# A hand-scheduled attention and FFN kernel: attention steps moved, five instruction streams put in a run-time loop, another warm-up

## The reference

```
a   = layernorm(x)
xn  = layernorm(a) * gamma + beta
q, k, v = split(xn @ w_qkv)            # 4 heads of 32
k   = softmax(k, over tokens);  q = q / sqrt(32)
att = (q @ (k^T v)) @ w_out + b_out + a
x   = x + layernorm(att)
f   = sum over 8 experts of (silu(n @ Wg) * (n @ Wu)) @ Wd,  n = layernorm(x)
x   = x + layernorm(f)
```

## Time and profile before

| what | value |
|---|---|
| median of 3 runs | 551.97 us |
| the profiled execution's time | 551.86 us |
| its span in the trace | 550.1 us, 8657 instructions |
| PE busy | 542.4 us |
| DVE busy | 446.2 us |
| ACT busy | 347.5 us |
| POOL busy | 168.4 us |

### The profile page before, as it was taken

The page is one execution under the profiler, slowest core; times in us unless marked ns, Lnnn a source line. Parts: engine busy times, 40 slices in busy tenths (PEclk is TensorE's granted clock), DMA queues, the critical chain, the costliest instruction groups (busy, mean ns, idle before and its releaser), DMA issues.

```text
span 550.1 us, 8657 instructions
## 1 busy us (share of the span) xinstructions
PE 542.4 (99%) x2633; PEld 467.3 (85%) x2633; DVE 446.2 (81%) x982; ACT 347.5 (63%) x626; POOL 168.4 (31%) x205
## 2 busy tenths in 40 slices
PE   9999999999999999999999999999999999999996
PEld 5687888888888888888888888888888888888885
DVE  5897897899769997799877988779976898778666
ACT  6778776756675566755658566675667555655554
POOL 4888691216203360034501335022520033001001
PEclk9999999999999999999999999999999999999999
DMA  5433020210102101111102011021010200010000
GB/s 176 143 88 115 20 58 2 77 44 15 59 0 78 57 20 40 40 37 59 43 16 73 24 40 58 0 78 39 20 39 1 77 20 21 19 40 0 21 1 19
DMA packets 28030, 24.47 MB, mean 44 GB/s; under 512 B 3024, under 2 KB 20944, under 8 KB 27984
## 3 DMA queue, kind: packets, MB, share of 16 engines
q1 hardware_dynamic: 27408, 23.73, 13.6%
q10 hardware_dynamic: 576, 0.20, 0.1%
HBM read 15.27 MB, written 8.65 MB: 43 GB/s over the span
## 4 chain that ended last, share of the span: by engine, by line
PE 94%; DVE 2%; ACT 1%; issue 1%; POOL 0%; POOLq 0%; DVEq 0%; ACTq 0%
PE gate_ps L1033 10%; PE acc_ps L1036 10%; PE acc_ps L1034 10%; PE gate_ps L1034 10%; PE gate_ps L1036 10%; PE acc_ps L1033 10%; PE up_ps L1034 10%; PE up_ps L1033 10%; PE up_ps L1036 10%; PE att_ps L1119 1%; PE att_ps L1130 1%; PE up_ps L1178 1%; PE att_ps L1092 1%; DVE h L839 0%; DVE h_lo L826 0%
## 5 line engine op out<-in xcount | busy, mean ns | idle before, releaser
L623 ACT ACTIVATE gs<-gate_ps 128x512 f32<-128x512 f32 x255 | 152.0, 596 | 175.6 <-PE gate_ps L1036 173.3
L839 DVE TENSOR_TENSOR h<-gs,up_ps 128x512 f32<-128x512 f32 x255 | 174.5, 684 | 90.5 <-PE up_ps L1036 88.7
L826 DVE TENSOR_TENSOR h_lo<-h,h_hi 128x512 fp32r<-128x512 f32 x255 | 195.6, 767 | 0.1
L600 ACT ACTIVATE h_hi<-h 128x512 fp32r<-128x512 f32 x255 | 158.9, 623 | 10.4 <-DVE h L839 9.9
L1033 PE MATMUL gate_ps<-x1nT_hi,wg_hi 128*128 128x512 f32 (+1 forms) x256 | 100.1, 391 | 0.0
L1036 PE MATMUL gate_ps<-x1nT_lo,wg_hi 128*128 128x512 f32 (+1 forms) x256 | 96.9, 379 | 0.0
L1033 PE MATMUL up_ps<-x1nT_hi,wu_hi 128*128 128x512 f32 (+1 forms) x256 | 96.9, 379 | 0.0
L1034 PE MATMUL gate_ps<-x1nT_hi,wg_lo 128*128 128x512 f32 (+1 forms) x256 | 96.9, 379 | 0.0
L1036 PE MATMUL up_ps<-x1nT_lo,wu_hi 128*128 128x512 f32 (+1 forms) x256 | 96.9, 379 | 0.0
L1034 PE MATMUL up_ps<-x1nT_hi,wu_lo 128*128 128x512 f32 (+1 forms) x256 | 96.9, 379 | 0.0
L1036 PE MATMUL acc_ps<-h_lo,wd_hi 128*128 128x512 f32 x254 | 96.6, 380 | 0.3 <-DVE h_lo L826 0.3
(11 more groups left out here) (238 smaller groups left out, 490.0 us busy)
## 6 DMA issues: line engine op xcount, KB each, us to landing
w_raw<-in_L_ffn_Wg_dram SPq DMA_DIRECT2D x8, 256.0 KB, 2.9
w_raw<-in_L_ffn_Wu_dram SPq DMA_DIRECT2D x8, 256.0 KB, 2.6
w_raw<-in_L_ffn_Wd_dram SPq DMA_DIRECT2D x8, 256.0 KB, 3.1
x_in<-in_L_attn_x_dram SPq DMA_DIRECT2D x7, 256.0 KB, 2.8
t_dram_acc<-t_blk_acc SPq DMA_DIRECT2D x7, 256.0 KB, 2.3
t_out_acc<-t_dram_acc SPq DMA_DIRECT2D x28, 64.0 KB, 2.0
out_dram<-res SPq DMA_DIRECT2D x7, 256.0 KB, 2.0
t_dram_x<-t_blk_x SPq DMA_DIRECT2D x6, 256.0 KB, 2.2
```

What stands on the lines that cost most here:

```text
L600: act.activation(h_hi[s % NH][:, :], h[s % NGU][:, :], ACT.Copy).then_inc(s_hhi, 1)
L623: act.activation(gs[q][:, :], gate_ps[q][:, :], ACT.Silu).then_inc(s_silu, 1)
L826: dve.tensor_tensor(h_lo[s % NH][:, :], h[s % NGU][:, :], h_hi[s % NH][:, :].bitcast(F32), ALU.subtract).then_inc(s_hlo, 1)
L839: dve.tensor_tensor(h[q][:, :], gs[q][:, :], up_ps[q][:, :], ALU.mult).then_inc(s_h, 1)
```

## The change

Three parts. The tables for batches 1 to 7 are rewritten; the FIRST tables stay. `bodies` becomes a run-time loop on each engine: batch 0 unrolled, a loop of two rounds with the bodies of an odd and an even batch (1 and 2, then 3 and 4), then batches 5, 6 and 7 unrolled; some waits are followed by an increment of a semaphore that nobody waits for, so that they are instructions of their own. And the warm-up ahead of the first body is 11 bf16 matmuls, a wait for the first weight part, 6 float32r matmuls with strided views of it and 2 bf16 matmuls, in place of 20 bf16 ones. SP issues the x1n transfers ahead of those of x, and ACT no longer waits for attn before it writes xnT.

```diff
-PE_AT = {"kT": 1, "A": 9, "M": 11, "G": 13, "attn": 14}
-DVE_AT = {"kmax": 2, "acc": 2, "E_T": 3, "next_stats": 6, "A": 10, "fin_stats": 10, "M": 12, "fin_scale": 12, "next_T": 14,
-          "z": 15, "z_stats": 15, "x1_stats": 20, "next_xnT_lo": 22, "x1n_T": 23, "x1n_lo": 29}
-ACT_AT = {"exp": 2, "G": 14, "next_xnT": 20, "next_xnT_hi": 21, "x1n_hi": 28}
-POOL_AT = {"yb": 4, "next_rstd": 7, "next_xn": 10, "fin_rstd": 11, "fin_out": 13, "z_rstd": 16, "x1": 16, "x1_rstd": 20}
-BUSY = {"start": 8, "w": 5, "attn": 20}
+PE_AT = {"kT": 1, "A": 9, "M": 10, "G": 11, "attn": 12}
+DVE_AT = {"next_xnT_lo": 31, "kmax": 2, "acc": 2, "E_T": 3, "A": 10, "fin_stats": 10, "M": 11, "fin_scale": 12, "z": 13, "z_stats": 13,
+          "next_stats": 16, "x1_stats": 18, "x1n_T": 21, "next_T": 24, "x1n_lo": 27}
+ACT_AT = {"exp": 2, "G": 12, "x1n_hi": 26, "next_xnT": 29, "next_xnT_hi": 30}
+POOL_AT = {"yb": 4, "fin_rstd": 11, "fin_out": 13, "z_rstd": 14, "x1": 14, "x1_rstd": 18, "next_rstd": 21, "next_xn": 21}
+BUSY = {"start": 8, "w": 5, "attn": 11, "end": 2}
...
-        def bodies(body):
-            for b in range(B):
-                body(b, b % 2, first=b == 0, nxt=b < B - 2, last=b == B - 1)
+        def wait_alone(eng, semaphore, value):
+            eng.wait_ge(semaphore, value)
+            eng.sem_inc(s_waited, 1)
+        def bodies(eng, body):
+            body(0, 0, first=True, nxt=True, last=False)
+            with eng.Fori(0, (B - 4) // 2) as i:
+                body(i * 2 + 1, 1, first=False, nxt=True, last=False)
+                body(i * 2 + 2, 0, first=False, nxt=True, last=False)
+            body(B - 3, 1, first=False, nxt=True, last=False)
+            body(B - 2, 0, first=False, nxt=False, last=False)
+            body(B - 1, 1, first=False, nxt=False, last=True)
...
         # SP body
                     store(b - 1)
+                    if not last:
+                        store_blocks("x1n", s_x1n_blk, b)
+                        load_blocks("x1n", b)
                 if nxt:
                     store_blocks("x", s_xh_blk, b + 1)
                     load_blocks("x", b + 1)
-                if not first and not last:
-                    store_blocks("x1n", s_x1n_blk, b)
-                    load_blocks("x1n", b)
...
         # POOL: power, scale_of (both waits) and next_xn; DVE: aggregate
-                pool.wait_ge(s_ve[k], count)
+                wait_alone(pool, s_ve[k], count)
-                dve.wait_ge(s_st[k], count)
+                wait_alone(dve, s_st[k], count)
...
         # ACT, next_xnT
-                    act.wait_ge(s_attn_ps, c - 1)
...
         # PE, ahead of the first body
             keep_busy(BUSY["attn"])
+            pe.wait_ge(s_whi, 1)
+            w0, w1 = w_hi[0][:, 0, :], w_hi[0][:, 0, 0:P]
+            forms = [w0.rearrange("p (a b) -> p b a", a=4), w0.rearrange("p (a b) -> p b a", a=8),
+                     w0.rearrange("p (b a) -> p a b", a=2)]
+            for moving in forms:
+                for _ in range(2):
+                    pe.matmul(up_ps[0][:, :], w1, moving, start=True, stop=True)
+            keep_busy(BUSY["end"])
```

More of the change, by code:

```diff
@@ L202, in build @@
         s_made = sem("s_made")
+        s_waited = sem("s_waited")
         s_mask = sem("s_mask")
@@ L425, in body @@
                     load_blocks("x", b + 1)
-                if not first and not last:
-                    store_blocks("x1n", s_x1n_blk, b)
-                    load_blocks("x1n", b)
-            bodies(body)
+            bodies(sp, body)
             sp.wait_ge(s_last_res, JH)
@@ L445, in scale_of @@
             def scale_of(k, c, dst, src, done, which=0, place=range(J)):
-                pool.wait_ge(s_rstd[k], c)
-                pool.wait_ge(s_nm[k], c)
+                wait_alone(pool, s_rstd[k], c)
+                wait_alone(pool, s_nm[k], c)
                 for j in range(J):
@@ L493, in body @@
                             if nxt:
-                                pool.wait_ge(s_A_ps, b + 1)
+                                wait_alone(pool, s_A_ps, b + 1)
                                 attention("xn", b + 2, par)
@@ L538, in _ @@
                 split_lo(pool, m)
-            bodies(body)
+            bodies(pool, body)
             for i in range(2):
@@ L687, in _ @@
             act.activation(blocks_of(x1nT_hi[0][:, :], 1), two(up_ps[2][:, HALF]), ACT.Copy).then_inc(s_x1nT_hi, 1)
-            bodies(body)
+            bodies(act, body)
             last_step()
@@ L993, in _ @@
                 dve.tensor_copy(x1[0][:, j, :], tile_banks[j][:, D:2 * D]).then_inc(s_f_x1, 1)
-            bodies(body)
+            bodies(dve, body)
             last_step()
@@ L1262, in _ @@
                     last.then_inc(s_f_n, 1)
-            bodies(body)
+            bodies(pe, body)
             last_step((B - 1) % 2)
```

## The result

| | before | after |
|---|---|---|
| median of 6 runs each | 552.09 us (551.83 to 552.37) | 555.94 us (555.61 to 556.38) |
| ratio | | 1.0069, 95% interval 1.0057 to 1.0083 |
| profiled execution: time, span | 551.86, 550.1 us | 555.68, 553.9 us |

A forecast was written before the change was run, and what follows sets the result against it. PE was taken as the bound, busy 542.4 of 550.1 us. 551.86 + 2.7 (M to G) + 0.4 (exp chain) + 0.1 (jump) + 0 (warm-up) = 555.1; the median's 0.1 more makes 555.2 us, range 551.5 to 558.2.

The forecast's parts named there:

- exp chain in the loop: Batches 1 to 4: the loop's register work delays the chain from exp to h_lo, and so PE; 0.4 us (0 to 1.2).
- jump back: End of the loop's first round: instruction fetch delays DVE and ACT, covered by their idle time; 0.1 us (0 to 2.7).
- Part 1: Batches 1 to 6: attention stages drawn together, G waits for M_sb behind fin_stats on DVE; 2.7 us (1.8 to 3.6).
- The sign that was named for it: PE waits 0.3 to 0.5 us for M_sb; period 65.9 in late unrolled batches, 66.0 in looped ones, against 65.43.
- Part 2: The next batch's x chain goes late, with SP's new order and ACT's dropped wait; covered by step distances, cost 0.
- rival B: The loop is dear: PE has no lead at the jump, or the exp chain costs 1.2; 557.9 or 558.7 us; chance 0.17.
- rival C: Faster: batch 0's single waits for Ek and h_lo go and G doesn't wait either; 550.8 us; chance 0.10.
- A (G doesn't wait): Not slower: M_sb is ready in time for G in batches 1 to 6, the 2.7 goes; 552.0 us; chance 0.18.
- Part 4: Warm-up before the first transposes: strided matmuls at 0.216 us cost 0; at double that, PE 0.8 late at most.

The follow-up runs named there:

- e9: The kernel before with the new tables, SP's new order and ACT's dropped wait, but fin_stats behind M_sb on DVE: 552.37 us, ratio 1.0001.
- e3: The new kernel with the old warm-up of 20 bf16 matmuls: 555.89 us, ratio 1.0065.
- e6: The kernel before with only the separate waits added, unrolled, old tables and old warm-up: 553.25 us, ratio 1.0017.
- e2: The new kernel with fin_stats moved from DVE's step 10 to 11, behind M_sb: 553.95 us, ratio 1.0029.
- e5: The kernel before with only the new tables, SP's order and ACT's dropped wait, unrolled, old warm-up: 553.38 us, ratio 1.0019.
- e7: The new kernel with ACT's bodies written out and the other engines looped: 555.51 us, one execution.
- e12: The kernel before with batch 0's A one step later on PE and M, G, attn two later: median 556.11 us (two sorts of times), ratio 1.0039.
- e10: The kernel before with A, M, G and attn of batch 0 one step later on PE: 551.79 us, ratio 0.9991.
- e11: As e10, with x_stats, x_rstd and xn of batch 0 also moved to step 4: 552.07 us, ratio 0.9998.

## Why the prediction was right, and where its sum was not

The forecast was 555.2, and 555.94 lies in its range and on its side. Its terms against what the runs give:

| term | forecast | measured |
|---|---|---|
| M to G, its separate wait included | 2.7 (1.8 to 3.6) | 2.0: 0.33 x 6 |
| exp chain in the loop | 0.4 (0 to 1.2) | 0 to 0.1: looped 65.78, unrolled 65.75 |
| jump back | 0.1 (0 to 2.7) | 0.9 |
| x chain late, SP's order, ACT's wait | 0 | 0 (e9) |
| warm-up | 0 (to 0.8) | 0 (e3) |
| batch 0, separate waits | not priced | 0.8 (e6) |

**Part 1** had the mechanism, the place and the number of batches right (e2, e9), and its size 0.12 per batch too high. In e5, without the separate waits, it is 0.2: G 0.09 late and 0.1 of weight loading behind it. I had 0.31 late. Two slips make the difference. M costs PE more than the 0.45 between the end of step 11 (175.56 + 9 x 0.216 = 177.50) and 177.95: the second matmul behind it comes late too, 0.32 behind the first. Before, the row next to those of the earlier trace rows shows it:

```profile
178.27 0.38 PE L1034 MATMUL gate_ps<-x1nT_hi,wg_lo 128*128 128x512 f32 x1
```

There this 0.10 fell into step 12, behind 177.95; with M ahead of step 11 it falls in front of G, so PE wants G at 178.05 (in e9, where G waits for nothing, it comes 5.33 behind A; A at 172.73 before and 5.33 make 178.06). And I took the start of the next DVE instruction, 177.85, for that of `M_sb`; but that h stands 0.18 behind `ve_fin`, and `M_sb` starts 0.08 behind it (179.04 and 179.12 above), so at 177.75, and ends at 178.10. 0.05 behind that is 178.15, 0.10 late, as measured. The separate wait was taken at 0.05 of 0 to 0.15 and is 0.12: the 0.16 of idle that stands ahead of the aggregation.

The sign that was named for it came weaker: G's wait of 0.22 does not stand in the list of PE's waits of the new kernel, and the periods are 65.75 and 65.78 where 65.9 and 66.0 were expected.

**Part 2** held: distances of many microseconds hide the whole x chain. **The register work** held at its lower end. **The warm-up** cost the start 0.31 (first gate matmul at 20.64 and not 20.3) and the end nothing (e3).

**The jump** is where the argument failed, not only a size. The step was: DVE resumes at 220.5, 0.9 late, and its and ACT's idle time covers that until the copy of `acc` two steps on. The place of the first hurry was right; the wait is exactly there, at 227 us. The lateness was not. DVE and ACT at the jump in the new kernel:

```profile
219.19 0.69 DVE L849 TENSOR_TENSOR h<-gs,up_ps 128x512 f32<-128x512 f32 x1 [0.65 <-PE up_ps L1046]
...
220.39 0.69 DVE L746 TENSOR_TENSOR xnT_lo<-xnT,xnT_hi 128x512 fp32r<-128x512 f32 x1
223.21 0.69 DVE L849 TENSOR_TENSOR h<-gs,up_ps 128x512 f32<-128x512 f32 x1 [2.13 <-PE up_ps L1046]
```

```profile
218.99 0.62 ACT L610 ACTIVATE h_hi<-h 128x512 fp32r<-128x512 f32 x1
221.29 0.60 ACT L633 ACTIVATE gs<-gate_ps 128x512 f32<-128x512 f32 x1 [1.68 <-PE gate_ps L1046]
223.46 0.63 ACT L610 ACTIVATE h_hi<-h 128x512 fp32r<-128x512 f32 x1 [1.56 <-issue]
```

h should have started a step of 1.94 behind 219.19, at 221.13; it came 2.08 late and not 0.9. Times here are 1.58 later than in the earlier trace rows (h of step 31 at 219.19, before 217.61). Counted from that h, I had DVE at the branch after 0.2 and on its way 2.7 later. It got there after 0.5 (219.7), its sequencer went on 3.1 later (222.8), and h started another 0.4 behind that: 1.1 us more in three parts. ACT stood twice: 2.5 at the branch, and 1.56 more behind one silu, at 221.9. The sequencers' own rows at the loop's line (duration ns min/median/max, first and last start):

```profile
L351 ACTq FUSED_REGOPS  x2: 68/70/73, 87.1 to 221.1; - x2
L351 DVEq FUSED_REGOPS  x2: 85/85/85, 88.2 to 222.8; - x2
...
L351 ACTq COMPARE_BRANCH  x2: 40/50/59, 218.6 to 351.1; - x2
...
L351 DVEq COMPARE_BRANCH  x2: 55/64/74, 219.7 to 352.2; - x2
```

The first branch is the jump back; the register sums (last start 221.1 and 222.8) are the first thing done behind it. The other three show no stand in these rows: PE's weight-load sequencer 216.7 and 217.0, GpSimd 203.4 and 203.6, SP 211.4 and 211.7.

The fetch itself was priced nearly right, 3.1 on DVE against the 2.7 of a small transfer; that ACT would stand a second time was not foreseen. Of DVE's 2.08 the idle time covers 1.7 (with DVE's jump alone, e7, PE waits 0.37), even more than the two gaps of 0.65 that I counted on; with ACT's two stands it is 0.79 and no longer 0.37, and the weight loading behind it adds the 0.1 that was priced in part 1 and not here. The rule of the Trainium skill ("Runtime: NRT & Kernel Launch", Instruction fetch mechanics), that a taken branch out of the resident pages stalls until they are fetched, agrees with the trace for DVE and ACT: 3.1 and 2.5 us at this jump. Whether the other three had their targets resident, no row shows. The rule didn't make rival B come true, which put the price on PE.

**Batch 0** was looked at only for what could be gained (rival C). There PE waits for others at several places, and the delays of the separate waits of GpSimd's norm chain go on to it. In the new kernel, PE's transposes of x1n:

```profile
80.67 0.99 POOL L460 TENSOR_SCALAR x1n<-x,nm_x,rstd_x 128x128 f32<-128x128 f32 x1
...
80.99 0.38 PE L1046 MATMUL acc_ps<-h_lo,wd_hi 128*128 128x512 f32 x1
...
81.71 0.44 PE L1095 MATMUL att_ps<-ident,x1n 128*128 128x128 f32 x2 [0.34 <-POOL x1n L460]
```

My sum counted 0.05 per wait on DVE's chain in batches 1 to 6 and none of GpSimd's in batch 0, where the list of waits says that nothing has room. This omission and the jump (1.6 short together) outweigh the 1.1 too much of part 1 and the exp chain. That the total is only 0.7 low is in part luck: errors of both signs cancel.

**The rivals.** A (G doesn't wait) is refuted by G's spacing in the new kernel and by e2, where it goes, C by batch 0. B was right that the jump costs, but not in its size or its engine.

## What to carry to other kernels

When a stage moves, write down the whole order on the engine that answers it: the chain here was safe on PE and lost 2 us because one operand was made behind another norm on DVE, and one entry moved in a table gives it back. A loop over long bodies can make an engine stand at the jump (here DVE and ACT), and what that does to the time is the stand less the idle time up to the next operand that the bound engine needs; with two rounds a prefetch hint took the stand away and brought a dearer one behind the exit. Small costs that are free in the steady state are paid in full where the start is already late, so price them there first.

## What the hardware showed that was not expected

**DVE sometimes stands for as long as GpSimd keeps going.** h_lo takes 0.68 us. In e12 it took 5.51, beside four splits of GpSimd (above), in e10 3.56 beside the end of one and two more (the timelines of GpSimd and of DVE):

```profile
57.78 1.28 POOL L335 TENSOR_TENSOR wd_lo<-w_raw,wd_hi 128x512 fp32r<-128x512 f32 x1
59.03 1.27 POOL L335 TENSOR_TENSOR wg_lo<-w_raw,wg_hi 128x512 fp32r<-128x512 f32 x1
60.26 1.27 POOL L335 TENSOR_TENSOR wu_lo<-w_raw,wu_hi 128x512 fp32r<-128x512 f32 x1
```

```profile
58.52 3.56 DVE L826 TENSOR_TENSOR h_lo<-h,h_hi 128x512 fp32r<-128x512 f32 x1
```

Both end 0.55 behind the last of GpSimd's run (62.71 and 63.26; 61.53 and 62.08); in e11 it was 3.57. The usual meeting is shorter. In the kernel before, DVE got through behind one split, 0.55 behind its end too, and the next split took 1.74 instead of 1.27:

```profile
56.63 1.27 POOL L335 TENSOR_TENSOR wd_lo<-w_raw,wd_hi 128x512 fp32r<-128x512 f32 x1
56.67 1.78 DVE L826 TENSOR_TENSOR h_lo<-h,h_hi 128x512 fp32r<-128x512 f32 x1
```

What decides between the two stayed open. The operation that makes `h`, which has one of its inputs (`up_ps`) in PSUM, doesn't show this: in e10 the one at 57.91 took 0.69 beside the first split. The Trainium skill ("SBUF — State Buffer", SBUF: two separate sides) says that DVE with two SBUF inputs and GpSimd take a shared port pair by an exclusive lock for a whole instruction. The trace before agrees. e10 to e12 go beyond it: there the loser waited through several instructions, and not for one.

**Strided operands from SBUF.** The warm-up in the new kernel:

```profile
16.57 2.83 PE L1276 MATMUL up_ps<-wg_hi 128*128 128x512 f32 x6
19.23 0.62 PE L1188 MATMUL up_ps<-warm 128*128 128x512 bf16 x2
19.69 0.38 PE L1280 MATMUL att_ps<-ident,x1n 128*128 128x128 f32 x2
```

Six matmuls from 16.57 to 19.23 are 0.44 each, at a granted clock of 1.00 (windows view of that stretch), double the 0.216 of the FFN's own strided operands. Theirs have neighbours 1 KB apart; these six have them 512, 256 and 8 bytes apart, two of each. Which of these strides is slow was not taken apart. Part 4 took a rule on PSUM access for operands that lie in SBUF, so neither spacing tests it. The upper bound of part 4 was the true one for them; it didn't reach the end of the kernel because batch 0 waits anyway.
